# Last expert layer: gate values of two token blocks brought to the expert rows by DMA instead of by matrix product

## The reference

```python
def _L1_ffn_ref(x, w_gate, w_g, w_u, w_d):
    scores = x @ w_gate
    topk_scores, topk_idx = jax.lax.top_k(scores, K)          # K = 2
    topk_probs = jax.nn.softmax(topk_scores, axis=-1)
    gating = jnp.sum(jax.nn.one_hot(topk_idx, E) * topk_probs[..., None], axis=-2)
    hidden = jax.nn.silu(jnp.einsum('bsd,edm->ebsm', x, w_g)) * jnp.einsum('bsd,edm->ebsm', x, w_u)
    expert_out = jnp.einsum('ebsm,emd->ebsd', hidden, w_d)
    return jnp.einsum('bse,ebsd->bsd', gating, expert_out)
```

## Time and profile before

| | |
|---|---|
| median of 3 runs | 749.14 us (749.04 to 749.33) |
| the profiled execution: its own time | 749.08 us |
| its span in the trace | 747.3 us |
| TensorE granted clock, mean | 0.996 |
| PE, DVE, ACT, POOL busy | 97%, 82%, 63%, 77% |
| the 44 steps: first gate projection to the last addition to X | 631.8 to 744.6 us |

### The profile page before, as it was taken

One profiled execution on the slowest core, in us unless ns is written; L12 is line 12 of the kernel. 1 busy time (PEld: TensorE's weight loads), 2 busy tenths in 40 slices (PEclk: granted clock), 3 DMA queues, 4 the chain that ended last, 5 costly groups with the idle time before them and its releaser, 6 DMA issues.

```text
span 747.3 us, 12514 instructions
## 1 busy us (share of the span) xinstructions
PE 726.0 (97%) x4202; PEld 469.6 (63%) x4202; DVE 616.2 (82%) x1305; ACT 469.9 (63%) x1067; POOL 578.0 (77%) x484
## 2 busy tenths in 40 slices
PE   8999999999999999999999999999799999999997
PEld 6665555555555555555555555476466699788885
DVE  8888999999999999999999999756788636876654
ACT  4367767767767767767767766745587822454443
POOL 6489989989989989989989999935588761445554
PEclk9999999999999999999999999999999999999999
DMA  6200000000000000000000000040000000000000
GB/s 154 82 1 1 1 2 1 2 3 1 1 3 2 1 2 2 1 1 2 2 2 3 1 2 2 1 114 4 1 1 1 1 2 1 0 1 16 0 15 28
DMA packets 36616, 8.70 MB, mean 12 GB/s; under 512 B 26581, under 2 KB 35814, under 8 KB 36553
## 3 DMA queue, kind: packets, MB, share of 16 engines
q1 hardware_dynamic: 35272, 7.80, 5.0%
q10 hardware_dynamic: 1280, 0.12, 0.1%
HBM read 6.53 MB, written 1.05 MB: 10 GB/s over the span
## 4 chain that ended last, share of the span: by engine, by line
PE 71%; POOL 13%; issue 10%; DVE 5%; ACT 1%; POOLq 0%; DVEq 0%
PE ps L1420 18%; PE ps L1464 16%; PE ps L1406 15%; POOL hid_lo L952 7%; PE ps L1475 4%; PE ps L1815 4%; PE ps L1448 4%; POOL nrm L934 2%; POOL hid L934 1%; PE ps L1393 1%; PE ps L1394 1%; PE ps L338 1%; DVE mx L1006 1%; POOL up_x L928 1%; DVE mx L1000 1%
## 5 line engine op out<-in xcount | busy, mean ns | idle before, releaser
L1006 DVE TENSOR_REDUCE mx<-ps 128x1 f32<-128x512 f32 x492 | 307.5, 680 | 26.7 <-PE ps L1406 24.2
L578 ACT ACTIVATE prob<-ps 128x512 f32<-128x512 f32 x512 | 267.9, 608 | 76.7 <-PE ps L1420 76.6
L1420 PE MATMUL ps<-q_cols,key 128*128 128x512 f32 x512 | 213.7, 421 | 0.8 <-ACT prob L578 0.8
L1406 PE MATMUL ps<-key,q_rows 128*128 128x512 f32 x512 | 201.0, 397 | 0.8 <-DVE key L992 0.5
L851 POOL TENSOR_TENSOR part<-part,prob 128x512 f32<-128x512 f32 x124 | 158.6, 1289 | 33.4 <-DVE part L1021 29.0
L1420 PEld LDWEIGHTS ps<-q_cols,key 128*128 128x128 f32 x512 | 95.6, 188 | 98.7 <-issue 49.9
L1464 PE MATMUL ps<-prob,val 128*32 128x512 f32 x1024 | 124.1, 598 | 0.0
L1406 PEld LDWEIGHTS ps<-key,q_rows 128*128 128x128 f32 x512 | 95.9, 188 | 20.1 <-DVE mx L1000 1.4
L851 POOL TENSOR_TENSOR part<-part,pair 128x512 f32<-128x512 f32 x64 | 95.5, 1492 | 0.1
L952 POOL TENSOR_TENSOR hid_lo<-hid,hid_hi 128x512 fp32r<-128x512 f32 x44 | 56.8, 1293 | 49.6 <-ACT hid_hi L735 49.6
L851 POOL TENSOR_TENSOR pair<-prob 128x512 f32<-128x512 f32 x64 | 82.3, 1285 | 1.9 <-ACT prob L578 1.9
(11 more groups left out here) (282 smaller groups left out, 1151.7 us busy)
## 6 DMA issues: line engine op xcount, KB each, us to landing
den<-den_sb SPq DMA_DIRECT2D x124, 2.0 KB, 2.1
X<-in_L_attn_h_t_dram SPq DMA_DIRECT2D x4, 256.0 KB, 4.2
out_dram<-X SPq DMA_DIRECT2D x4, 256.0 KB, 2.3
w_raw<-in_L_ffn_w_g_dram SPq DMA_DIRECT2D x1, 704.0 KB, 4.4
w_raw<-in_L_ffn_w_u_dram SPq DMA_DIRECT2D x1, 704.0 KB, 6.2
w_raw<-in_L_ffn_w_d_dram SPq DMA_DIRECT2D x1, 704.0 KB, 8.0
w_o<-in_L_attn_W_O_dram SPq DMA_DIRECT2D x1, 512.0 KB
w_out<-in_L_attn_W_out_dram SPq DMA_DIRECT2D x1, 512.0 KB, 5.0
```

The costliest lines, as they stand in the source:

```text
L578: act.activation(prob[:, g % RING, :], ps[:, g % 3, :], ACT.Exp, scale=SCALE).then_inc(s_exp, 1)
L1006: dve.tensor_reduce(mx[:, n % 2, c % TPB, at:at + 1], ps[:, BANK["rows", 2 * lin + j], :], AX.X, ALU.max).then_inc(s_mrd, 1)
L1406: pe.matmul(ps[:, BANK["rows", 2 * lin + j], :], q_rows[:, k, i * P:(i + 1) * P], key[:, h % KBUF, c0:c0 + BLK], start=True, stop=True).th ...
L1420: pe.matmul(ps[:, g % 3, :], key[:, n // NB % KBUF, t * P:(t + 1) * P], q_cols[:, n % NB, :], start=True, stop=True).then_inc(s_sc, 1)
```

## The change

For steps 22 to 40 (blocks 2 and 3, but for the last three chunks of block 3) `gates(n)` is not run on TensorE. ScalarE writes the transposed gate values of blocks 2 and 3 to `gT_rows` (8 partitions); SyncE stores a block of them to a DRAM tensor `g_rows`, waits until that has landed, and then, for each step, loads `g_all[:, n % 6, :]`, 128 partitions of 512 values, with one DMA for each expert in the chunk (source: one DRAM row, read again for each partition by a stride of zero). `hid(n)` then takes the gate values from `g_all` in SBUF instead of from PSUM. A load into a slot of the ring of six waits for `hid(n-6)`. The ring's semaphores are ones that are used at the kernel's start. For block 3 ScalarE writes the values to `gT` as well, for the last three chunks; `gates_lo` of block 2 is dropped. The stores of blocks 0 and 1 to the output are issued between the loads of steps 28 and 29, and of 39 and 40.

```diff
+        GB, GR, G_LAST = 2, 6, 3
+        gT_rows = sb("gT_rows", [E, (NB - GB) * BLK])
+        g_rows = nc.dram_tensor("g_rows", [E, (NB - GB) * BLK], F32, kind="Internal").ap()
+        g_all = sb("g_all", [P, GR, BLK])
+        ld_grow, GROW0 = ld_k, 16 * N_LD_K
+        ld_gall, GALL0 = ld_x + [ld_u, ld_q], [16] * NB + [16 * N_LD_U, 16 * N_LD_Q]
+        def by_product(n):
+            return n < GB * CH or n >= NS - G_LAST
+        def pieces(c):
+            first, behind = c * P, (c + 1) * P
+            return [(e, max(e * M1, first) - first, min((e + 1) * M1, behind) - first)
+                    for e in range(E) if e * M1 < behind and (e + 1) * M1 > first]
@@ sync
-                for b in range(NB):
+                def store(b):
                     sp.wait_ge(s_x4, b + 1)
                     sp.dma_start(out_v[:, TPB * b:TPB * (b + 1), :], X[:, TPB * b:TPB * (b + 1), :]).then_inc(s_out, 16)
+                for n in range(GB * CH, NS - G_LAST):
+                    b, c = n // CH, n % CH
+                    if c == 0:
+                        cols = slice((b - GB) * BLK, (b - GB + 1) * BLK)
+                        sp.wait_ge(s_gt, b + 1)
+                        sp.dma_start(g_rows[:, cols], gT_rows[:, cols]).then_inc(ld_grow, 16)
+                        sp.wait_ge(ld_grow, GROW0 + 16 * (b - GB + 1))
+                    if n >= GB * CH + GR:
+                        sp.wait_ge(s_hid, n - GR + 1)
+                    for e, r0, r1 in pieces(c):
+                        sp.dma_start(g_all[r0:r1, n % GR, :], g_rows[e:e + 1, cols].to_broadcast([r1 - r0, BLK])).then_inc(ld_gall[n % GR], 16)
+                    if n == GB * CH + GR:
+                        store(0)
+                    elif n == GB * CH + GR + CH:
+                        store(1)
+                store(NB - 2)
+                store(NB - 1)
@@ scalar, gates_hi
-                    act.copy(gT[0:E, b * BLK:(b + 1) * BLK], ps[0:E, GATE_BANK[b], :]).then_inc(s_gt, 1)
+                    if b < GB:
+                        act.copy(gT[0:E, b * BLK:(b + 1) * BLK], ps[0:E, GATE_BANK[b], :]).then_inc(s_gt, 1)
+                        return
+                    if b == NB - 1:
+                        act.copy(gT[0:E, b * BLK:(b + 1) * BLK], ps[0:E, GATE_BANK[b], :])
+                    act.copy(gT_rows[:, (b - GB) * BLK:(b - GB + 1) * BLK], ps[0:E, GATE_BANK[b], :]).then_inc(s_gt, 1)
@@ vector, gates_lo
+                    if b == 2:
+                        return
@@ vector, the steps
-                    dve.wait_ge(s_bp, n + 1)
+                    if by_product(n):
+                        dve.wait_ge(s_bp, sum(by_product(x) for x in range(n + 1)))
+                        gates_of = ps[:, 4 + n % 2, :]
+                    else:
+                        dve.wait_ge(ld_gall[n % GR], g_count(n))
+                        gates_of = g_all[:, n % GR, :]
-                    dve.tensor_tensor(hid[:, n % 2, :], ps[:, 4 + n % 2, :], prod[:, n % 2, :], ALU.mult).then_inc(s_hid, 1)
+                    dve.tensor_tensor(hid[:, n % 2, :], gates_of, prod[:, n % 2, :], ALU.mult).then_inc(s_hid, 1)
@@ tensor
-                        gates(n)
+                        if by_product(n):
+                            gates(n)
```

More of the change, by code:

```diff
@@ L55, in build_kernel @@
         CH = E * M1 // P
+        NS = NB * CH
         assert E == 8 and 2 * BN == P and 2 * A == P and E * M1 == CH * P
@@ L378, in build_kernel, with g_count @@
         y_T = sb("y_T", [P, BLK])
+        GB, GR, G_LAST = 2, 6, 3
[10 more added lines that the diff above has]
+                    for e in range(E) if e * M1 < behind and (e + 1) * M1 > first]
+        def g_count(n):
+            return GALL0[n % GR] + 16 * sum(len(pieces(x % CH)) for x in range(GB * CH, n + 1) if x % GR == n % GR)
         s_gp, s_up, s_bp, s_sil, s_pr1, s_hid, s_hhi, s_hlo = (sem(n) for n in ("s_gp", "s_up", "s_bp", "s_sil", "s_pr1", "s_hid", "s_hhi", "s_hlo"))
@@ L381, in build_kernel @@
         sp_f = spread[:, :, :].rearrange("p e m -> p (e m)")
-        NS = NB * CH
         DLAG = 3
@@ L1844, in gates_T @@
                         pe.wait_ge(s_d1, 3 * GATE_STEPS + READ_SCORES)
-                    elif b >= 2:
-                        pe.wait_ge(s_gtl, b)
+                    elif b == 2:
+                        pe.wait_ge(s_gtl, 2)
+                    elif b == 3:
+                        pe.wait_ge(s_gt, 3)
                     for i in range(TPB):
@@ L1862, in gates @@
                         pe.wait_ge(s_gtl, b + 1)
+                    elif n == NS - G_LAST:
+                        pe.wait_ge(s_gtl, 3)
                     pe.matmul(ps[:, 4 + n % 2, :], sp_f[:, c * P:(c + 1) * P], gT[:, b * BLK:(b + 1) * BLK],
@@ L1930, in _ @@
                             if o == 0:
-                                pe.wait_ge(s_gtl, NB)
+                                pe.wait_ge(s_gtl, 3)
                             else:
```

## The result

| | before | after |
|---|---|---|
| median of 10 runs each | 749.02 us (747.96 to 749.52) | 744.42 us (743.48 to 748.38) |
| ratio, 95% interval | | 0.9948 (0.993 to 0.9966) |
| profiled execution, its span | 749.08, 747.3 us | 743.53, 741.8 us |
| first gate projection (step 0) to the first product of the last down projection (step 43) | 631.56 to 741.59 = 110.03 us | 630.52 to 736.04 = 105.52 us |

The kernel is 4.6 us faster by the medians; the interval of the ratio is 2.5 to 5.2 us. The profiled executions are 5.5 us apart, but only 4.51 of it lies in the steps; 1.04 us was already there when step 0 began (631.56 against 630.52; the table ahead of the prediction has 631.8 for the first, which is 0.2 too late).

A forecast was written before the change was run, and what follows sets the result against it. The prediction took TensorE's number of products per step as the bound. From 749.08 us it subtracted 4.41 us for 19 gate products, all other terms 0, giving 744.7 us, range 744.0 to 748.0.

The forecast's parts named there:

- TensorE sets the pace, 0.232 us a product: Steps 22 to 40: 19 gate products of 0.232 us removed, 4.41 us saved; a step falls from 2.32 to 2.09 us.
- DMAs at nothing: Added stores and 19 loads of 256 KB: issued and landed early enough, so cost 0.
- Rival 3: Loads of gate values too slow, 4.1 us each at 64 GB/s: 12 us late, 757 us; chance 0.03.
- ScalarE's copy and the dropped `gates_lo` at nothing: ScalarE's extra 0.57 us copy in steps 11 to 13 is covered by slack; gates_lo(2) leaves VectorE, which has room: 0.
- The lock between `hid` and `hid_lo`: Steps 22 to 40: VectorE's hid and GpSimd's hid_lo can't overlap; first hid 0.93 us late, two steps 4.26 us; cost 0.
- the cover: Time by which hid_lo ends before its down projection: 2.4 us at 2.09 us steps, against at most 1.7 us of lateness.
- Rival 1: GpSimd's hid_lo(n) starts before VectorE's hid(n+1): 2.56 us a step, net +2.6, 751.7 us; chance 0.10.
- Rival 2: Order of hid and hid_lo mixed: six to ten steps GpSimd first, or slower hid, 745.6 to 747.6 us; chance 0.14.
- the bad order: GpSimd's hid_lo(n) ahead of VectorE's hid(n+1): 2.56 us a step instead of 2.09, 0.47 lost each time.

The follow-up runs named there:

- the square of four kernels: Changed kernel and variants, all with loads: gate products dropped or all kept, hid's operand from SBUF or PSUM; steps 105.54 and 105.53 us dropped, 110.03 and 110.04 kept.

## Why the prediction was right

The forecast was 744.7 us, in the range 744.0 to 748.0; measured 744.42. That the median comes within 0.3 us is partly luck: the ten runs go from 743.48 to 748.38 us, with granted clocks from 1.000 to 0.989, and the sum started from a profile that had lost 1.04 us ahead of the steps. What tests the sum is the time of the steps.

**TensorE sets the pace, 0.232 us a product.** Right. The steps lost 4.51 us against 4.41; per product that is 0.237. The down projections start 2.08 us apart in steps 23 to 40, predicted 2.09, with one of about 2.5 in each block for the transposes, as before. From step 22 on TensorE idles ahead of the last two down projections alone, 0.24 and 0.69 us (before 0.23 and 0.68). The whole gain belongs to the products, as the square of four kernels shows. The 2.08 us are nine products of 0.231; the tenth was worth 0.237, a little more than its share.

**DMAs at nothing.** Right. Landing in 1.6 to 4.9 us with 12.5 of lead. SP issued at 0.42 us a piece (predicted 0.4); the store of `g_rows` for block 3 with its wait held SP from 698.40 to 701.03, 2.6 us (predicted 3), and nobody waited. Rival 3 is out, and even with a third of the lead, in the ring of two, the loss is 1.8 us.

**ScalarE's copy and the dropped `gates_lo` at nothing.** Right. No idle time of TensorE appears in steps 0 to 21 that before has not, and the kernels with all products, where ScalarE makes the second copy for two blocks, have the steps of before.

**The lock between `hid` and `hid_lo`.** The step on which the prediction hung. Predicted: first `hid` 0.93 us late; measured duration 1.60 instead of 0.69, 0.91. Predicted: in a pair VectorE is ahead by 0.1 us; measured 701.59 and 701.69. Predicted: 4.26 us for two steps; measured 4.28. Predicted: the cover is used up but for 0.7 us; the least room measured in steps 22 to 40 was at step 33, where `hid_lo` ended at 716.29 and its down projection began at 716.88, 0.59 us. The timeline around it (the stretched `hid_lo` began at 714.54 and took 1.75):

```profile
714.54 1.75 POOL L997 TENSOR_TENSOR hid_lo<-hid,hid_hi 128x512 fp32r<-128x512 f32 x1 [1.28 <-ACT hid_hi L780]
...
716.88 0.39 PE L1907 MATMUL ps<-hid_hi,w_hi 128*128 128x512 f32 x1
```

The 0.7 was right partly because two errors cancel. The cover is not 2.4 us but 2.17, as the kernel with the PSUM operand has it in plain steps: the prediction shortened two of the three steps of lag by 0.24 us, and all three are shorter. And against that kernel `hid_lo` was at most 1.57 us late (step 33), not 1.7: the delay grows by 0.12 to 0.13 us a pair and not 0.08, but it doesn't add up over 19 steps, as it falls to 0.1 us or less at each of the two `y_T` copies.

That the lag of three steps is what hides it, I had only argued; the three kernels at a lag of two show it: there the same lock costs 3.8 us and the change gains nothing.

The rule of the Trainium skill ("SBUF — State Buffer", section "Who interferes with whom") holds in this kernel too: with the PSUM operand `hid` and `hid_lo` overlap and take 0.69 and 1.30 us, with the SBUF operand the later one is held until the other is done. Whether the time matters was decided here by the lag: it cost 0.0 us at three steps and 3.8 at two.

**Rivals.** Rival 1, GpSimd first in every step, did not come in the changed kernel. Of its 19 `hid` nine are held (1.60 to 1.67 us) and never two in a row; at the two `y_T` copies (692.38 and 715.69) two in a row are free. Rival 2 needed six or more steps in the bad order; there was none. But both live close by, and their price was sized well: in the ring of two rival 1's order held for five steps at 2.58 us each (2.56 in the prediction), and at a lag of two a mixture came. With the ring of six and the lag of three the 0.1 us by which VectorE is first was enough every time.

**What was off.** Beside the two terms of the cover above, sizes in the experiments: that the cost at a lag of two would be 1.2 to 2.4 us (3.8), that the kernel before would bear a lag of two (it lost 5.6 us), and that no product left would be a draw (0.8 us worse). Each time I had summed the first delay and not what a waiting TensorE does next: it holds back its own later work, and may lose its clock.

## What to carry to other kernels

When TensorE is the bound, a product that only copies or spreads values onto rows can be given to DMAs: here each one removed gave 0.24 us, and 5.0 MB of broadcast loads cost nothing. Before moving an operand from PSUM to SBUF, look at what GpSimd runs beside that instruction, add up both engines' times as if they were one (here 1.70 us of a 2.08 us step), lay out who comes first (the same two instructions take 2.14 us a step in one order and 2.58 in the other), and check how many steps of lag hide the delay. And read the durations too: an engine held in this way looks busy and not idle.

## What the runs showed of the hardware that was not expected

- TensorE's granted clock fell to the lower of its two levels (1.2 GHz) after an idle time within the steps. In the kernel with no product left it idled 2.0 us (737.67 to 740.09 less the last product's time), and the next products came 0.43 us apart at a granted clock of 0.53:

```profile
740.00:743.00 3.00, 2.90 (x6) 1.67 (x6) 0.00 (x0) 0.00 (x0) 1.27 (x2) 0.53 0.00 0
```

  At a lag of two, an idle time of 2.7 us ahead of the first down projection was followed by some eight products at 0.43 us in two of the three kernels; the third, with the same idle time, kept 0.23. The changed kernel idles 1.08 us ahead of its first down projection, and its products after it kept 0.23. So the fall after an idle time of 2.7 us is not certain; what decides it stays open here.
- The exact size of the lock: a held VectorE sum or product of 128x512 ends 0.55 us after the other's end, a held GpSimd one 1.15 us. In the kernel before's attention stage it is 0.54 to 0.55 in all 34 cases of the one kind and 1.14 to 1.16 in all 31 of the other, and the steps have the same (688.26 + 1.60 = 689.86, 0.55 after `hid_lo` ended at 689.31). Alone the two take 0.69 and 1.29 us, so about 0.14 us of a held instruction passes before the other is done. A start 0.01 us earlier was enough to be the one that is not held (704.49 against 704.50 in the kernel with all products and the SBUF operand).
